# New order of every engine's steps in a 32-batch decoder kernel, and a second buffer for one scaled column

## What is computed

```python
x = layernorm(x + attn(x))            # stage a and b: gated delta rule, then a mixture of experts
x = layernorm(x + xattn(x, ctx, ctx)) # stage b and c: 16 heads of 16
x = layernorm(x + ffn(x))             # stage c: 16 columns, top 1 of them

# attn: zrms, qkvz = x @ W (256 x 3072), causal conv of 4 taps over 2048 channels, silu,
#       beta = sigmoid(b), g = -exp(A) * softplus(a + dt), then per head (8 of 128 x 128)
S = S * exp(g_t); delta = (v_t - k_t @ S) * beta_t; S = S + outer(k_t, delta); o_t = q_t @ S
#       rms norm, gate with silu(z), W_out, residual; router with top 2 of 8 experts of 128
# ffn:  top 1 of 16 columns of 64 by softmax, gelu(x @ W_cols) * weight @ proj_w + x
```

## Time and profile before

| | us |
|---|---|
| median of 3 runs | 2283.04 (2275.72 to 2289.95) |
| profiled execution | 2278.91 |
| its span, first to last instruction | 2277.1 |
| TensorE busy (weight loads) | 2016.3 (1714.4) |
| VectorE, ScalarE, GpSimd busy | 1542.3, 1448.9, 1033.9 |
| mean granted TensorE clock | 0.938 |

### The profile page before, as it was taken

The page is one execution under the profiler, slowest core; times in us unless marked ns, Lnnn a source line. Parts: engine busy times, 40 slices in busy tenths (PEclk is TensorE's granted clock), DMA queues, the critical chain, the costliest instruction groups (busy, mean ns, idle before and its releaser), DMA issues. The chain is left out here.

```text
span 2277.1 us, 57052 instructions
## 1 busy us (share of the span) xinstructions
PE 2016.3 (89%) x20842; PEld 1714.4 (75%) x20842; DVE 1542.3 (68%) x4652; ACT 1448.9 (64%) x4290; POOL 1033.9 (45%) x2741
## 2 busy tenths in 40 slices
PE   4588998999899899899889899889999999989976
PEld 3477887777787777788777788777788777778864
DVE  3467677777767767776767776766777777776643
ACT  3366666766666776666676666676666677665542
POOL 1435544444554444454444454444455444455421
PEclk8699999999999999999999999999999999999986
DMA  6100110010011001011001011001011000101000
GB/s 224 16 12 12 17 17 11 12 17 15 14 17 17 10 13 17 12 17 17 14 10 17 12 17 17 14 10 17 12 17 17 15 10 15 17 12 17 15 4 5
DMA packets 228470, 43.91 MB, mean 19 GB/s; under 512 B 212032, under 2 KB 225360, under 8 KB 227424
## 3 DMA queue, kind: packets, MB, share of 16 engines
q1 hardware_dynamic: 228192, 40.28, 9.4%
HBM read 29.62 MB, written 10.62 MB: 18 GB/s over the span
## 5 line engine op out<-in xcount | busy, mean ns | idle before, releaser
L1066 DVE SCALAR_TENSOR_TENSOR acc<-ypad,convw,acc 128x128 f32<-128x128 f32 x1536 | 490.0, 385 | 20.4 <-ACT acc L868 20.3
L505 PE MATMUL bank_a<-xnT,wqkvz 128*128 128x128 f32 x2048 | 256.6, 280 | 4.0 <-DVE u L1142 4.0
L505 PEld LDWEIGHTS bank_a<-xnT,wqkvz 128*128 128x128 f32 x2048 | 247.1, 196 | 7.4 <-issue 5.9
L1361 POOL TENSOR_TENSOR rqk<-sse,nhalf 128x8 f32<-128x8 f32 x32 | 53.6, 1675 | 409.5 <-DVE sse L1071 409.5
L1491 POOL TENSOR_SCALAR lnv<-mv 128x1 f32<-128x1 f32 x128 | 29.4, 229 | 408.7 <-DVE mv L1156 405.9
L979 ACT ACTIVATE prob<-bank_b,nmax 128x128 f32<-128x128 f32 x512 | 182.9, 386 | 4.8 <-DVE nmax L1216 3.6
L1418 POOL TENSOR_TENSOR wsub<-wsub,tsub 128x112 f32<-128x112 f32 (+6 forms) x448 | 139.9, 312 | 35.1
L1142 DVE SCALAR_TENSOR_TENSOR u<-bank_a,ostat,zs 128x128 f32<-128x128 f32 x256 | 71.7, 342 | 124.0 <-POOL ostat L1451 124.0
L1415 POOL TENSOR_TENSOR tsub<-lsub,wsub 128x112 f32<-128x112 f32 (+6 forms) x448 | 133.1, 297 | 32.6
L868 ACT ACTIVATE acc<-bank_a,convw 128x128 f32<-128x128 f32 x512 | 146.2, 379 | 0.0
L518 PE MATMUL bank_a<-wqkvz,xnT 128*128 128x512 f32 x256 | 124.1, 608 | 14.6 <-DMA bk<-in_bk_dram 14.6
(11 more groups left out here) (253 smaller groups left out, 5505.4 us busy)
## 6 DMA issues: line engine op xcount, KB each, us to landing
xin<-in_x_dram SPq DMA_DIRECT2D x32, 128.0 KB, 2.4
lower_rows<-diag SPq DMA_DIRECT2D x32, 128.0 KB, 2.3
lsub<-lower_rows SPq DMA_DIRECT2D x128, 32.0 KB, 2.1
cin<-in_ctx_dram SPq DMA_DIRECT2D x32, 128.0 KB, 2.1
zraw<-inverse_rows SPq DMA_DIRECT2D x32, 128.0 KB, 2.3
out_dram<-yout SPq DMA_DIRECT2D x32, 128.0 KB, 1.7
wqkvz<-in_wqkvz_dram SPq DMA_DIRECT2D x6, 512.0 KB, 7.1
inverse_rows<-wsub SPq DMA_DIRECT2D x128, 16.0 KB, 1.9
```

What stands on the lines that cost most here:

```text
L505: last = mm(A[bank][:, b * P:(b + 1) * P], wqkvz[:, c, o:o + P], xnT[:, c, :], start=(c == 0), stop=(c == KC - 1))
L1066: stt(acc[:, c, :], ypad[:, c, k:k + P], convw[:, c, k:k + 1], acc[:, c, :], ALU.mult, ALU.add).then_inc(conv.sem, 1)
```

## The change

Two things. The five lists of `ORDER` are new; and `ckk` becomes `ckk2`, two buffers by turns, so that `a_sc` of batch n waits for `a_zin` of batch n - 2. No step is added or left out, and no step's instructions change. The wait is now made from batch 3 on.

```diff
 ORDER = dict(
-    pe="b_w1@2 b_cT@2 a_z1@1 a_vT0@1 a_qk@1 b_x2T@2 b_v@2 b_router@2 b_gu0@2 b_gu1@2 b_gu2@2 b_gu3@2 a_xT "
...
+    pe="b_w1@2 b_cT@2 a_qkv3@1 a_qk@1 b_x2T@2 b_v@2 b_router@2 a_vT0@1 b_gu0@2 b_gu1@2 b_gu2@2 a_xT b_gu3@2 "
...
-        ckk = sb("ckk", [P, HV])
+        ckk2 = [sb(f"ckk{i}", [P, HV]) for i in range(2)]
...
-                    last = tt(diag[r, :, :], kkT[r, :, r], cols(ckk[r, :], BLK), ALU.mult)
+                    last = tt(diag[r, :, :], kkT[r, :, r], cols(ckk2[n % 2][r, :], BLK), ALU.mult)
...
-                    tt(heads(zin, half), heads(zraw, half), cols(ckk[:, 4 * half:4 * half + 4], BLK), ALU.mult)
+                    tt(heads(zin, half), heads(zraw, half), cols(ckk2[n % 2][:, 4 * half:4 * half + 4], BLK), ALU.mult)
...
-                if not first(n):
-                    pool.wait_ge(*z_ok(n - 1, 2)).then_inc(passed.sem, 1)
-                tt(pairs(ckk[:, :]), pairs(krb[:, :]), rk, ALU.mult).then_inc(kscale.sem, 1)
+                if n > 2:
+                    pool.wait_ge(*z_ok(n - 2, 2)).then_inc(passed.sem, 1)
+                tt(pairs(ckk2[n % 2][:, :]), pairs(krb[:, :]), rk, ALU.mult).then_inc(kscale.sem, 1)
```

More of the change, by code:

```diff
@@ L113 @@
 ORDER = dict(
-    pe="b_w1@2 b_cT@2 a_z1@1 a_vT0@1 a_qk@1 b_x2T@2 b_v@2 b_router@2 b_gu0@2 b_gu1@2 b_gu2@2 b_gu3@2 a_xT "
[3 rows of a table removed]
+    pe="b_w1@2 b_cT@2 a_qkv3@1 a_qk@1 b_x2T@2 b_v@2 b_router@2 a_vT0@1 b_gu0@2 b_gu1@2 b_gu2@2 a_xT b_gu3@2 "
[3 rows of a table added]
        "c_pj1 b_w0".split(),
[L119 to L123, removed]
[3 rows of a table removed]
[L127 to L130, removed]
+    act="c_c0@3 c_te@3 c_wT@3 c_c1@3 a_z1@1 b_oT0@2 a_qkv2@1 b_oT1@2 b_sum@2 a_mix2@1 b_cT@2 a_qkv3@1 b_x2T@2 "
+       "b_rl@2 a_z0@1 a_sum b_rt@2 b_sg0@2 a_xT a_mix3@1 b_sg1@2 a_ba a_ln a_seg a_qkv0 a_qkv1 a_dec1 "
+       "b_y1T@2 a_dec0 a_mix0 a_mix1 b_q@2 a_sq c_exp0 a_st c_exp1 c_exp2 c_exp3 c_pT0 c_pT1 a_zf@1 a_zo@1 "
+       "c_R a_mt@1 a_sz0@1 a_sz1@1 c_y2T a_o0@1 c_h a_o1@1 c_lt".split(),
+    dve="c_gc0@3 c_gc1@3 c_weight@3 a_conv20@1 a_conv21@1 a_conv22@1 c_sum3@3 b_hid@2 c_y3@3 b_x2@2 b_v@2 "
[3 rows of a table added]
+       "c_sum2 c_y2 c_lb a_core0@1 c_route c_y4@3 a_core1@1".split(),
+    pool="a_osc1@2 c_y2b@3 a_sub0@1 a_sub1@1 c_ln2@3 b_rs@2 c_ln3@3 b_xh@2 a_xr@1 a_sub2@1 a_x b_rd@2 b_rt@2 "
+       "a_ga a_rq@1 a_g b_ln0@2 a_sc b_y1b@2 b_mask c_ln1 c_rx a_osc0@1 c_sig".split(),
+    sp="a_in@1 c_out@4 a_w1@1 a_w2@1 b_in a_l1 a_l2".split(),
 )
@@ L1110, in a_zin @@
                 for half in range(2):
-                    tt(heads(zin, half), heads(zraw, half), cols(ckk[:, 4 * half:4 * half + 4], BLK), ALU.mult).then_inc(z_ok.sem, 1)
+                    tt(heads(zin, half), heads(zraw, half), cols(ckk2[n % 2][:, 4 * half:4 * half + 4], BLK), ALU.mult).then_inc(z_ok.sem, 1)
                 for half in range(2):
```

## The result

The changed kernel took 2213.95 us (median of 4 runs, 2209.39 to 2222.45) against 2280.4 (median of 4) for the one before on the same chip: a ratio of 0.971, with 0.966 to 0.975 as its interval. It is faster by 66 us, where 63 were forecast (2220 against 2283).

What follows compares the result with a forecast made beforehand. Each trip was taken as bound by a ring of TensorE, VectorE and ScalarE pieces: 36.5 + 13.85 + 12.65 + 1.1 + 0.5 = 64.6, plus 0.8 clock, 65.4 us. 2278.9 - 57.4 - 1.2 = 2220 us; range 2190 to 2285.

Steps and rivals of the forecast that it cites:

- The ring and its three pieces: Each trip is a ring of pieces set by TensorE, VectorE and ScalarE in turn; 64.6 us before the clock.
- The new wait: On TensorE before `c_s` (L735 or L739), for `kT` or `qT`: a gap of 2.0 to 2.8 us.
- VectorE's piece: From `b_dn0` to the last of 24 taps: 13.85 us, with `b_k` and two maxima gone from it.
- TensorE's piece: From `c_xo` to `b_dn0`: 36.23 us before, 36.5 forecast.
- One sign: ScalarE would have no pause from `b_q` to the last `c_pT`.
- GpSimd in VectorE's way: Rival, no chance given: first eight taps beside `gseg` cost 0.6 us more; trip 66.0, total time 2238 us.
- The place of `a_ba`: On TensorE, moved ahead of `b_dn0`: 0.52 us less its overlap, +0.37 us on the stretch from `c_xo`.
- The clock term: Half clock behind the gap before `c_s`: half a step, 0.8 us a trip, bounds 0 and 2.5.
- the gap only moves: Rival, chance 0.19: TensorE waits as long before `c_s`, clock falls as often; trips 66.6 to 68, about 2275 us.
- slower, through the clock: Rival, chance 0.12: half clock falls behind `c_xo`, 3.2 us on 65.1; trip 68.3, total time 2305 us.
- The first trips: Start-up: packing of `wq` and `wk` moves into GpSimd's wait for the first `lsub`; 1.2 us off, up to 2.2.
- The rule on table loads: About 2.66 us per ScalarE table switch, with a drain: trip 66.8, total time 2260 us; the sum used 1.30.

Runs made afterwards that it cites:

- the second half alone: New order only from `b_dn1` to `c_xo`, old order elsewhere, against the kernel before: ratio 0.988 (0.984–0.991), mean trip 66.71 us.
- one buffer: The new order with a single `ckk` and its wait for the batch before, against the kernel before: ratio 0.974 (0.970–0.978), mean trip 65.75 us.
- the first half alone: New order only from `c_xo` to the down products, old order in the rest, two buffers, against the kernel before: ratio 0.998 (0.995–1.000), mean trip 68.10 us.

## Why the prediction was right, and where it was off

**The ring and its three pieces held.** The wait before L580 went, one came before L735 for `kT`, and ScalarE had no pause before the exponentials. The new wait is 1.64 in a usual trip, shorter than the 2.0 to 2.8 forecast, mostly because VectorE's piece is 0.54 shorter. TensorE's piece is 36.38 (36.5 forecast), VectorE's 13.31 (13.85), what is left beside ScalarE's 1.59 (1.58). One sign failed: ScalarE was to have no pause from `b_q` to the last `c_pT`, and it waits before L894 in 28 batches (29.4 us in total).

**VectorE's piece was 0.54 too long,** because all taps run at 0.27 us each, where I had taken over the 0.31 of the first eight and the 0.35 of the next four. Before, these twelve ran while GpSimd was at `gseg` and the product behind it:

```profile
1962.63 2.75 POOL L1428 TENSOR_SCALAR gseg<-const,gate 128x128 f32<-128x128 f32 x4 [0.21 <-POOL gate L1425]
1965.67 1.39 DVE L1066 SCALAR_TENSOR_TENSOR acc<-ypad,convw,acc 128x128 f32<-128x128 f32 x4
```

Now `gseg` is all but over when they start. GpSimd and VectorE in a usual trip:

```profile
1576.48 2.37 POOL L1428 TENSOR_SCALAR gseg<-const,gate 128x128 f32<-128x128 f32 x4 [0.21 <-POOL gate L1425]
1578.55 2.19 DVE L1066 SCALAR_TENSOR_TENSOR acc<-ypad,convw,acc 128x128 f32<-128x128 f32 x8
```

It ends at 1578.85, 0.30 into the first taps, and the eight still take 0.27 each. The rival "GpSimd in VectorE's way" did not come true: it had the first eight taps beside `gseg` at 0.385, and the mean of a tap over the run went down, 385 to 364 ns. That GpSimd is what slows a tap is the likely reading; no run moved `gseg` alone.

**The place of `a_ba` was costed on one side only.** The prediction booked it as a loss of 0.37 on TensorE, and that is what it costs there (36.38 against 36.01). It is also worth 1.95 us of VectorE's piece, and 1.0 of the trip in all, since `a_seg` ahead of `a_qkv0` puts a wait for GpSimd's `gate` (0.59) and `a_seg` itself (1.28) between the gates' two tables and the taps. The 13.85 was right only because this move was in the change; nothing in the working would have said so without it, and my miss on the second half alone is the same hole.

**The clock term was half of what it is.** The step that failed: "A step that falls behind the new gap meets work that ScalarE holds back anyway, so I take half a step, 0.8". It doesn't. TensorE at half clock is late with `a_ss`, and ScalarE waits for it before L894, in the middle of its own piece: 14.24 on average, 12.84 with the gap filled (12.65 forecast). With eight products in the gap that wait is left in 2 batches of 32. The clock costs a trip 65.49 - 63.96 = 1.5, twice my 0.8 and about the full step of 1.58 of the earlier trace rows. It stayed inside the bounds of 0 and 2.5. Two errors cancelled: 64.6 + 0.8 = 65.4 forecast, 64.0 + 1.5 = 65.5 found. The right total was in part luck.

**TensorE's idle time as the cause of half clock** is shown by filling the gap with work, in either order. It is not that one gap as such: with `b_k` and `b_q` early only 0.40 of it was left, and the idle time behind it did the same. The rival "the gap only moves" named something real: the gap did move, and the clock went on falling behind it. But 66.6 to 68 didn't come as the mean trip: at full clock the new order is 2.2 us shorter, and half clock takes 1.5 from it where it took 1.3 from the old one. The rival "slower, through the clock" had its price nearly right (68.3) and its frequency wrong: trips of 67.7 and 67.9 exist at 0.92, 2 of 29 in the changed kernel; with `b_k` early there are 18 of 29 at 0.92. The 65.1 that it adds its 3.2 to is derived nowhere in the prediction. The Trainium skill (TensorE: Matmul & The Clock Gate, HAM oscillation) tells of a kernel that waits for a DMA in each tile and starts each tile cold. These traces show something like it with TensorE busy 91% of the span: waits of 1.64 us for another engine, and half clock in 25 of 29 trips.

**The first trips** gave 7.3 where 1.2 was forecast. The second trip went from 61.59 to 55.82. Kernels with the same lists there differ by their clock: it takes 56.0 at 0.86 with three products in the gap, and 58.1 to 58.4 at 0.81 to 0.82 with one, with eight, or with one buffer. So 2.3 to 2.6 of the 5.8 come and go with the clock of the execution. TensorE's waits in it, before:

```profile
112.33 6.41 PE L505 MATMUL bank_a<-xnT,wqkvz 128*128 128x128 f32 x32 [4.03 <-DVE u L1142]
120.94 3.72 PE L651 MATMUL bank_b<-wout,prob 128*128 128x256 f32 x16 [1.33 <-ACT prob L939]
```

And after:

```profile
110.89 2.02 PE L505 MATMUL bank_a<-xnT,wqkvz 128*128 128x128 f32 x16 [2.35 <-DVE u L1142]
114.03 4.00 PE L651 MATMUL bank_b<-wout,prob 128*128 128x256 f32 x16 [0.25 <-ACT prob L939]
```

In the young pipeline `a_qkv2` and `a_qkv3` stood together behind `core`; now one has moved to behind `b_cT`, which I had booked as "change places at equal length". The third batch starts at 138.0 with the second half alone, at 131.1 with the first half alone, so the gain belongs to the first half's lists; which of their moves makes how much of it was not tried. The end, 4.5 us shorter, was not looked into.

**The rule on table loads** (the Trainium skill, ScalarE: Activation LUTs, What ACT_TABLE_LOAD costs) would have given 2260 by its 2.66 us a switch. The load before the exponentials still takes 1.30 to the next activation (1522.55 to 1523.85 in the trip above), with no drain to be seen.

## What to carry to other kernels

Cut a steady trip at the few events where the work passes from one engine to another, and cost a move by each piece that it lengthens or shortens, down to the chain that feeds the piece's first instruction. The longest wait in the list is not the bound (removing it by itself made this kernel 1.1% slower), and a step of half a microsecond can hold up two. Then look at the granted clock by trip; if TensorE shows half clock behind the same gap each time, try a few products that nobody reads in that gap before reordering anything: 0.8 us of them gave 2% here. And price half clock at its full length wherever another engine waits for what TensorE does there.

## What the hardware showed that I had not expected

Half clock in a kernel whose TensorE is busy 89 to 91% of the time, in all but four of 29 trips of the changed one: 1.3 to 1.5 us a trip, some 2% of the whole. Three products of 512 columns in a gap of 1.64 us took it away in all 29 trips; one product didn't (4 trips at 1.00 with and without it). The same instructions gave trips from 63.66 to 67.91 us in one execution, in no order that I could read.

A tap of 128 x 128 on VectorE took 0.27 us behind GpSimd's `gseg`, 0.31 beside it and 0.35 in the four taps after that; over a whole run of the changed kernel the mean is 0.36, so elsewhere in the trip taps are slower still. What slows them was not taken apart.
